# A transformer tower on one core: products on zeros at the start, routers in two halves, the class token's attention a group later, heads not divided

## What is computed

```python
h = tok(x)                    # x (4, 3, 512, 192): sin and cos of 2*pi*x*freq (6 bands), times W (6912 x 192)
h = concat([cls_tok, h])      # 4 batches of 513 positions, 192 wide
h = h + attn(layernorm(h))
h = h + ffn(layernorm(h))

def attn(x):                  # gated linear attention over 64 features
    q, k = (elu(x @ Wq) + 1) * 64 ** -0.5, elu(x @ Wk) + 1
    c = clip(cumsum(log(sigmoid(x @ Wf + bf))), -20, 20)
    heads = (q . exp(c) * cumsum(exp(-c) k v)) / ((q . exp(c) * cumsum(exp(-c) k)) + 1e-6)
    return (layernorm(heads) * gamma + beta) @ Wo

def ffn(x):                   # 8 experts, 2 for each position, and a shared one
    routed = sum over the top 2 of softmax(x @ router_w) of gate * (silu(x @ w_gate) * (x @ w_up)) @ w_down
    shared = (silu(x @ ws_gate) * (x @ ws_up)) @ ws_down
    a = sigmoid(x @ sg_w + sg_b)
    return a * shared + (1 - a) * routed
```

## Time and profile before

| | |
|---|---|
| median of 3 executions | 557.06 us (554.62, 557.3, 557.06) |
| the profiled execution | 554.62 us, its span 552.8 us |
| TensorE busy | 535.8 us (97% of the span) |
| VectorE busy | 370.3 us (67%) |
| ScalarE busy | 244.4 us (44%) |
| GpSimd busy | 180.3 us (33%) |
| DMA, mean | 77 GB/s |

### The profile page before, as it was taken

How to read it: one execution, slowest core, us unless ns; L and a number is a source line. 1 busy time by engine, 2 the same in 40 slices (tenths; PEclk the granted TensorE clock), 3 DMA queues, 4 the chain that set the end, 5 groups by cost and what they waited for, 6 DMA issues and landing times.

```text
span 552.8 us, 9034 instructions
## 1 busy us (share of the span) xinstructions
PE 535.8 (97%) x3235; PEld 504.8 (91%) x3235; DVE 370.3 (67%) x1065; ACT 244.4 (44%) x343; POOL 180.3 (33%) x205
## 2 busy tenths in 40 slices
PE   5999999999999999999999999999999999999997
PEld 5998999899999899999989999978877899999865
DVE  8637787534868637978853995468998256666437
ACT  3465464755324764243565422264142135555410
POOL 6413134122234311765212460002601414444510
PEclk9999999999999999999999999999999999999999
DMA  8900067000000001110000010510103441531174
GB/s 330 341 23 20 7 219 250 20 10 20 20 19 21 20 0 27 62 59 0 1 1 10 20 59 1 185 54 30 50 0 125 157 136 47 171 99 51 52 216 142
DMA packets 23488, 42.49 MB, mean 77 GB/s; under 512 B 2502, under 2 KB 15044, under 8 KB 23348
## 3 DMA queue, kind: packets, MB, share of 16 engines
q1 hardware_dynamic: 19560, 33.31, 18.4%
q0 software_dynamic: 3472, 8.07, 4.1%
q10 hardware_dynamic: 412, 0.53, 0.4%
HBM read 31.74 MB, written 14.79 MB: 84 GB/s over the span
## 4 chain that ended last, share of the span: by engine, by line
PE 80%; DVE 11%; ACT 4%; issue 2%; DMA 1%; ACTq 0%; DVEq 0%
PE ps L1369 44%; PE ps L1571 3%; PE ps L1624 2%; PE ps L1626 2%; PE ps L1533 1%; PE ps L1602 1%; PE ps L1603 1%; PE ps L1604 1%; PE ps L1606 1%; PE ps L1605 1%; DMA r<-r 1%; PE ps L1537 1%; PE ps L1535 1%; PE ps L1536 1%; PE ps L1534 1%
## 5 line engine op out<-in xcount | busy, mean ns | idle before, releaser
L1369 PE MATMUL ps<-w_tok,feat 128*128 128x192 f32 x1728 | 289.4, 328 | 7.5 <-ACT feat L502 6.2
L1369 PEld LDWEIGHTS ps<-w_tok,feat 128*128 128x128 f32 x1728 | 282.9, 191 | 8.7 <-issue 8.7
L426 POOL TENSOR_SCALAR feat<-fx 128x512 int32<-128x512 f32 x108 | 93.4, 880 | 189.4 <-PE ps L1369 185.8
L511 ACT ACTIVATE feat<-feat 128x1536 f32<-128x1536 f32 x35 | 52.0, 1485 | 110.1 <-DVE feat L805 110.1
L801 DVE SCALAR_TENSOR_TENSOR feat<-fx,feat 128x512 f32<-128x512 f32 x105 | 76.5, 781 | 1.8 <-POOL feat L426 1.5
L462 POOL DMA_INDIRECT ydram<-yr,xs x39 | 37.8, 969 | 53.9 <-DVE yr L1127 53.9
L514 ACT ACTIVATE feat<-feat,half_pi 128x1536 f32<-128x1536 f32 x35 | 54.6, 1561 | 0.0
L456 POOL DMA_INDIRECT slots<-pay_a,posi x17 | 17.4, 1025 | 75.2 <-DVE posi L1053 71.8
L805 DVE TENSOR_SCALAR feat<-feat 128x1536 int32<-128x1536 int32 x35 | 37.3, 1066 | 1.2
L1571 PE MATMUL ps<-w_down,hid_ring 128*128 128x192 f32 x192 | 35.4, 328 | 2.2 <-DVE H L1085 2.2
L616 ACT ACTIVATE s_ring<-ps 128x512 f32<-128x512 f32 x24 | 14.4, 599 | 52.4 <-PE ps L1537 52.4
(11 more groups left out here) (306 smaller groups left out, 859.6 us busy)
## 6 DMA issues: line engine op xcount, KB each, us to landing
slots<-in_blank SPq DMA_DIRECT2D x1, 5031.0 KB, 19.2
w_tok<-in_wT SPq DMA_DIRECT2D x7, 576.0 KB, 8.9
fx<-in_xT SPq DMA_DIRECT2D x15, 256.0 KB, 2.7
xs<-slots SPq DMA_DIRECT2D x5, 645.0 KB, 5.8
yin<-ydram SPq DMA_DIRECT2D x8, 384.0 KB, 6.6
raw_a<-in_wea SPq DMA_DIRECT2D x4, 384.0 KB, 5.4
raw_b<-in_web SPq DMA_DIRECT2D x4, 384.0 KB, 6.0
w_tok<-in_wT SPq DMA_DIRECT2D x4, 288.0 KB, 7.5
```

Of the source, the lines that this page charges most:

```text
L426: ins = pool.tensor_scalar(feat[:, k % SLOTS, i, :].bitcast(I32), x[:, x_block(k), :], f_col[:, fi:fi + 1], 1.0, ALU.mult, ALU.mult)
L511: act.activation(feat[:, k % SLOTS, 0:3, :], feat[:, k % SLOTS, 0:3, :], ACT.Sin, scale=TWO_PI).then_inc(sin_ready, 1)
L1369: ins = pe.matmul(ps[:, TOK[a % 2][t // 2], (t % 2) * D:(t % 2 + 1) * D], feat[:, k % SLOTS, i, t * P:(t + 1) * P], w_tok[:, k, i, :], sta ...
```

## The change

It has these parts:

- `run_in`: eight products of 128x128 by 128x192 zeros on TensorE before everything; the zeros are a row of `pay_a[1]`, whose memset moves to the front of VectorE's list.
- The second group's first feature gets a remainder and a sine of its own (`second_remainders`).
- In the opening, the class token's steps from `attn2` on VectorE and ScalarE, from `attn3` on TensorE, move one group later. The class token's router goes from ahead of group 8 to behind it.
- Heads are not divided. Layernorm of heads / d is computed as layernorm of the heads with an epsilon of 1e-5 times d squared; `attn5` reads them from PSUM.
- The second copy of the normalised columns (128 to 191) is made by ScalarE (`twice`) for batches 1 to 3; for the class token and the last batch it stays on VectorE behind the first.
- In the batches 1 to 3, `log_odds` stands ahead of `sines(b, 4)` on ScalarE, and `negatives` and `clip_odds` ahead of `gates` on VectorE.
- `router` on TensorE has two halves of two tiles each with other work between them. `down(18)` goes one tile later.

The diff, cut to its core:

```diff
@@ scalar, sines @@
+                if q == 1:
+                    act.wait_ge(abs_second, 1)
+                    act.activation(feat[:, 1, 0, :], feat[:, 1, 0, :], ACT.Sin, scale=TWO_PI).then_inc(sin_second, 1)
+                    act.wait_ge(r_ready, 2)
+                    act.activation(feat[:, 1, 1:3, :], feat[:, 1, 1:3, :], ACT.Sin, scale=TWO_PI).then_inc(sin_ready, 1)
...
+            def twice(a):
+                act.wait_ge(xn2_ready, a + 1)
+                act.activation(payload(a)[:, :, D:XD], payload(a)[:, :, P:D], ACT.Copy).then_inc(twice_ready, 1)
@@ scalar, order of the opening and of batches 1 to 3 @@
             sines(0, 3)
+            sines(0, 4)
             act.wait_ge(consts_ok, 2)
             attn2(0)
-            sines(0, 4)
             sines(0, 5)
+            sines(0, 6)
             attn6(0)
             split_hi_piece(0)
-            sines(0, 6)
+            sines(0, 7)
             split_hi_piece(1)
-            sines(0, 7)
+            sines(0, 8)
             attn8(0)
-            sines(0, 8)
             sines(1, 0)
             router(0)
             take_h(0)
...
                 take_v(b, 0)
+                log_odds(b)
                 sines(b, 4)
                 take_v(b, 1)
-                log_odds(b)
                 powers(b)
@@ vector, layernorm @@
+                    if over is not None:
+                        for lo, d in over:
+                            n = d.shape[1]
+                            ins = dve.tensor_scalar(den[0:TP, lo:lo + n], d, DEN_EPS, None, ALU.add)
...
+                        ins = dve.scalar_tensor_tensor(den2[0:TP, 0:nt], den[0:TP, 0:nt], LN_EPS, den[0:TP, 0:nt],
+                                                       ALU.mult, ALU.mult)
...
+                        next_(dve.tensor_tensor(v_, mv[0:TP, 0:nt, 1], den2[0:TP, 0:nt], ALU.add))
@@ vector, order of the opening @@
             first_remainders()
-            remainders(0, 1)
+            second_remainders()
             attn0(0)
...
             remainders(0, 3)
+            remainders(0, 4)
             attn2(0)
-            remainders(0, 4)
+            remainders(0, 5)
             attn3(0)
             make_state()
             attn5(0)
-            remainders(0, 5)
+            remainders(0, 6)
             attn6(0)
-            remainders(0, 6)
             split_piece(0)
+            remainders(0, 7)
             attn7(0)
-            remainders(0, 7)
             split_piece(1)
+            remainders(0, 8)
             attn8(0)
             dve.wait_ge(split_done, SP_)
             dve.memset(spare[0:DB, 0, :], 0.0)
-            remainders(0, 8)
             remainders(1, 0)
             router(0)
@@ tensor @@
+            def run_in():
+                pe.wait_ge(blank_ready, 1)
+                for _ in range(RUN_IN):
+                    pe.matmul(ps[:, A0, 0:D], pay_a[1][:, NT, 0:P], pay_a[1][:, NT, 0:D], start=True, stop=True)
...
+            run_in()
             project(0, 0)
...
             project(0, 3)
+            project(0, 4)
             attn3(0)
             attn5(0)
-            project(0, 4)
+            project(0, 5)
             attn6(0)
-            project(0, 5)
+            project(0, 6)
             attn7(0)
-            project(0, 6)
+            project(0, 7)
             attn8(0)
-            project(0, 7)
+            project(0, 8)
             pe.wait_ge(router_split, 2)
-            router(0)
-            project(0, 8)
+            router(0, 0)
+            router(0, 1)
...
-                project(b, 0)
+                project(b, 0, range(3))
+                if b >= 2:
+                    router(b - 1, 0)
+                project(b, 0, range(3, 6))
                 attn1(b)
                 if b >= 2:
-                    router(b - 1)
+                    router(b - 1, 1)
...
-            router(B - 1)
+            router(B - 1, 0)
             for q in range(NQB):
-                up(q)
+                up_one(q, 0)
+                if q == 0:
+                    router(B - 1, 1)
+                up_one(q, 1)
...
                 if q == Q_LG:
-                    router(B)
+                    router(B, 0)
                 if q == Q_RK:
                     ranks(B)
                 if q >= 2:
                     down(q - 2)
+                if q == Q_LG:
+                    router(B, 1)
...
-                if i == 1:
-                    down(NQB - 1)
                 if 2 <= i < NTILE + 2:
                     tile_hidden_t(i - 2)
+                if i == 2:
+                    down(NQB - 1)
```

More of the change, by code:

```diff
@@ L592, in attn8 @@
                 xh_a_, _, xh_b_, _ = operands(a)
+                if 1 <= a < B:
+                    twice(a)
                 act.wait_ge(xpose3, a + 1)
@@ L758, in _, with layernorm @@
         def _(dve):
-            def layernorm(src, dst, a, which, TP, nt, done, twice=False, parts=(0, 1, 2)):
+            def layernorm(src, dst, a, which, TP, nt, done, over=None, parts=(0, 1, 2)):
                 n0 = (3 * a + which) * LNS
@@ L825, in attn0 @@
                     dve.wait_ge(h_ready, a)
-                layernorm(residual(a), normed(a), a, 0, TP, nt, xn_ready, parts=parts)
+                layernorm(tiles_of(residual(a), TP), normed(a), a, 0, TP, nt, xn_ready, parts=parts)
             def attn1(a):
@@ L943, in norm_rest @@
                     dve.wait_ge(scat, scattered(a - 2))
-                layernorm(residual(a), payload(a), a, 2, TP, nt, xn2_ready, twice=True, parts=parts)
+                layernorm(tiles_of(residual(a), TP), payload(a), a, 2, TP, nt, xn2_ready, parts=parts)
+                if 2 in parts and a in (0, B):
+                    for i in range(nt):
+                        ins = dve.tensor_scalar(payload(a)[:, i, D:XD], residual(a)[0:TP, i, P:D], mv[0:TP, i, 0:1],
+                                                y[0:TP, i:i + 1], ALU.subtract, ALU.mult)
+                    ins.then_inc(twice_ready, 1)
             def attn8(a):
@@ L1274, in _ @@
                 if q == Q_LN2:
-                    divide(B)
-                    norm_heads(B)
+                    attn5(B)
                 if q == Q_X2:
@@ L1494, in attn8, with router @@
                 ins.then_inc(xpose3, 1)
-            def router(a):
+            def router(a, half):
                 W, TP, nt = width(a)
                 xh_a_, xl_a_, xh_b_, xl_b_ = operands(a)
-                pe.wait_ge(xh_ready, a + 1)
-                pe.wait_ge(xl_ready, a + 1)
-                if a >= 1:
-                    pe.wait_ge(dz_ready, a)
-                for i in range(nt):
+                if half == 0:
+                    pe.wait_ge(xh_ready, a + 1)
+                    pe.wait_ge(xl_ready, a + 1)
+                    if a >= 1:
+                        pe.wait_ge(dz_ready, a)
+                for i in range(half * nt // 2, (half + 1) * nt // 2):
                     o, c = ps[0:TP, logit_bank(a), 16 * i:16 * i + NR], slice(i * P, i * P + TP)
@@ L1509, in router @@
                     ins = pe.matmul(o, xl_b_[:, c], wrb[:, :], start=False, stop=True)
-                ins.then_inc(lg_psum, 1)
+                if half == 1:
+                    ins.then_inc(lg_psum, 1)
             def ranks(a):
```

91 lines of the change are left out of this document (48 added, 43 removed).

## The result

The changed kernel took **561.75 us** (median of four runs, 561.38 to 562.81) against 556.93 us for the kernel before (554.62 to 557.3): a ratio of 1.0096, 95% interval 1.0069 to 1.0123. It is slower by 1%, and lies above the forecast of 558.9 and above its range, which ended at 561.5. The profiled execution took 562.81 us, 8.2 more than the 554.62 of the one before, where the sum had +3.3.

A forecast was written before the change was run, and what follows sets the result against it. TensorE, busy 535.8 of 552.8 us, was taken as the bound. Terms -2.0 -1.3 -0.9 +1.3 +1.5 +3.9 +0.8 = +3.3 on 554.62 give 557.9; 1.0 for slower executions makes 558.9 us, range 554.0 to 561.5.

The forecast's parts named there:

- Products on zeros, -2.0: Start: eight products raise TensorE's clock before the first sine; 2.0 us saved, at most 2.2, possibly no gain.
- Class token's attention later, -1.3: Opening: TensorE's wait of 1.1 us ahead of group 4 and 0.2 ahead of group 7 go.
- new waits of 1.3 and 1.5 us: Opening: TensorE waits for late sines ahead of groups 7 and 8, behind the weight splits; 1.3 and 1.5 us added.
- The wait for `xn`, +3.9: Batch 1, ahead of `attn1(1)`: layernorm comes late behind the class token's moved router; TensorE waits 3.9 us.
- The clock in that wait: Rival, batch 1: TensorE's clock falls in the 3.9 us wait, 2.2 us more, 561.1 us; chance 0.15.
- Keys' copy, -0.9: Batches 1 to 3: earlier logarithm removes TensorE's waits on the keys' copy and weight loads alongside; 0.9 us saved.
- Halves in the last batch, +0.8: Last batch: `down(9)` between the router's halves completes logits later and delays `ranks`; 0.8 us added (0.3 to 1.3).
- Last batch's other savings, 0: Last batch: shorter `attn5` and vanished waits gain nothing, since `finish(0)` starts where it did; bound -1.4 us.
- The unexplained 2.4 us: Excess of slower executions of the kernel before; low clock at the start guessed as cause, 1.0 us carried into forecast.
- Heads not divided, and the second copy on ScalarE, 0: Batches 1 to 3: VectorE saves 1.3 + 0.9 us a batch, but TensorE waits for neither; 0 us.
- The three named tests: Signs of error: `xn` wait under 2 us, 528 ns records behind 93 us, last batch's waits shrinking over 1 us together.

The follow-up runs named there:

- `ln_and_splits`: Changed kernel with class token's router behind batch 1's layernorm, weight splits behind groups 7 and 8's sines, last router whole, `down(18)` at its old place: 551.11 us.
- `pool_held`: Changed kernel with GpSimd's conversions for group 3 of batch 1 held until VectorE's layernorm has made `xn`: 560.25 us.
- `log_alone`: Kernel before with only the logarithm ahead of the sines, and `negatives` and `clip_odds` ahead of `gates`: ratio 0.9998.
- `halves_alone`: Kernel before with only TensorE's routers in two halves, at all places: 555.63 us.
- `ln_splits_finish`: `ln_and_splits` with GpSimd's first two `e_lo` one position later in the last stage's planner table: 549.75 us.
- `ln_first`: Changed kernel with the class token's router on ScalarE and VectorE behind batch 1's layernorm, TensorE's order kept: 554.72 us.
- `filled_wait`: Changed kernel with 16 more products on zeros on TensorE ahead of the `xn` wait in batch 1: 560.08 us.
- `best_halves`: `ln_and_splits` with the last batch's router in halves again and `down(18)` at its later place: 552.33 us.
- `run_in_alone`: Kernel before with only the products on zeros, memset first, and the second group's finer steps: 554.31 us.
- `opening_alone`: Kernel before with only the opening's order: class token's attention a group later, its router behind group 8: 564.66 us.

## Why the prediction was wrong

The sum had the right waits in the right places. One of its terms was too small, the wait for `xn`, and one that it left out came true, the clock in that wait; the second was a rival with a chance of 0.15. The smaller misses are in the list.

- **Products on zeros, -2.0**: right. -2.2 in the trace, -1.5 alone at the full clock, +1.5 when left out. No row had priced it before; the low bound of no gain did not come true. Their 16 records take 4.53 us and not 5.1, since the clock rises among them.
- **Group 2**: not forecast, a wait of 0.44 us. TensorE arrives 2.2 us earlier, and only the second group's chain was given finer steps. It stands in three of the eight traces with products on zeros, so it belongs to the execution as much as to the change.
- **Class token's attention later, -1.3**, and **new waits of 1.3 and 1.5 us** ahead of groups 7 and 8: 0.97 and 1.26 by the rows, and the table is within 0.3 us of the forecast up to batch 1's first group. `ln_and_splits` shows the cause.
- **The wait for `xn`, +3.9**: the step that failed in size. It measured 5.0. I took the layernorm's 5.2 us from the earlier trace rows, between two conversions of GpSimd; later by some 5 us the same steps lie beside GpSimd's conversions. `pool_held` gave 3.7.
- **The clock in that wait**: the step that failed in kind. I gave the fall 0.15; it happened in all four executions, and after 3.7 us of idling in five of six. Its price was near the 2.2 I gave: 1.7 between medians, 2.8 in the profiled execution. My argument was that the trace had no fall after a wait of 1.1 us, which says nothing of 4. The one long idle stretch that the trace did have, the 6.2 us at the start, ends at the low clock; I set it aside as being the start. The Trainium skill ("TensorE: Matmul & The Clock Gate", "HAM oscillation — how this bites in real kernels"), which I quoted against the change, warns of a clock that falls in idle gaps between stages; the traces agree, with the clock at 0.50 behind waits of 5.0 and 3.7 us.
- **Keys' copy, -0.9**: 1.1 alone by medians. In the traces of both `log_alone` and the changed kernel only some 0.55 stays: 0.8 shows up to the keys' products of batch 3, and new gaps of 0.28 us ahead of the state's products in batches 2 and 3 take back a part each time. I had put the cost of the sines behind the logarithm at 0.
- **Halves in the last batch, +0.8**: 0.7 at `ranks` in the traces of `halves_alone` and of the changed kernel, and 0.9 up to the end of the latter, where `down(18)` trades a wait of 0.5 us for one of 0.7. **Last batch's other savings, 0**: right, and `ln_splits_finish` shows what swallowed them.
- **The unexplained 2.4 us**: I laid them to the low clock at the start and carried 1.0. Wrong cause. They are falls of the clock behind whole routers, which the halves remove (none below 0.998 in 32 executions of the four kernels with halves everywhere and without an idle wait, `ln_first`, `filled_wait`, `halves_alone` and `best_halves`) and products on zeros do not. The changed kernel's 561.75 is therefore to be read against the full-clock 554.8: +3.3 as forecast, +1.1 for the longer wait, +1.7 for the clock, and 0.9 that is left. In the traces 0.3 of this lies in the opening and 0.4 in the keys' part.
- **Heads not divided, and the second copy on ScalarE, 0**: no run has either alone. No wait of TensorE on them shows in the trace, and VectorE's and GpSimd's busy times fell.

The three named tests came out as: `xn` wait over 2 us, as forecast; records at half speed behind 93 us, which I had written down as the sign of being wrong; the last batch's waits not smaller.

## What to carry to other kernels

A step that moves past a group must be followed to the first thing that TensorE needs from that engine, and its duration taken beside what GpSimd will be doing at the new time, not at the old. A new idle stretch of some microseconds on TensorE costs itself and then the clock; filling it with products on zeros gives back the clock (1.7 of 7.0 us here), moving the late step gives back all of it. When executions of one kernel differ, read each one's mean clock before comparing medians: the logarithm's move looked like nothing (ratio 0.9998) until the like were compared (1.1 us at the full clock).

## What the runs showed of the hardware

- The clock fell with TensorE busy by every record: 0.3 to 1.3 us behind 2.2 us of 20 products of 10 columns each (`run_in_alone`, `log_alone`, `opening_alone`, `ln_and_splits`), in some executions and not in others of the same program. With the same products in two halves it did so in none of the 12 of `halves_alone`. Why one execution falls and another does not stays open.
- After an idle stretch the clock fell in all four executions of the changed kernel (5.0 us) and in five of six of `pool_held` (3.7 us).
- Products on zeros raise the clock: the 96 records behind them took 15.84 to 16.10 us in eight traces, against 17.90 to 18.52 in five without. And they hold it (`filled_wait`, granted clock 1.00 in all of the wait).
- VectorE's steps on 128 x 4 values took 0.60 to 0.63 us beside GpSimd and 0.16 to 0.17 without (`pool_held`).
